# Embedding lookup, two interaction layers and a small MLP: a third low part by the adding DMA, 14 tiles split, rows in DRAM by chunks, second top weights loaded late

## The reference

```
x1[b,o,d] = relu(sum_{h,m} W1[o, 32h+m] * e[b,h,d] * e[b,m,d] + b1[o])        o < 128; h, m < 32
x2[b,o,d] = relu(sum_{h,m} W2[o, 32h+m] * x1[b,h,d] * e[b,m,d] + b2[o])       h < 64; m < 32
z = [sum_d x1[b,64:128,d], sum_d x2[b,:,d]], joined with the 16 dense inputs: 208 numbers
y = relu(relu(z W_top1 + b_top1) W_top2 + b_top2) W_top3
```

## Time and profile before

| | |
|---|---|
| median of 3 runs | 2021.38 us |
| profiled execution | 2020.18 us |
| its span, first to last instruction | 2018.4 us |
| PE busy | 1991.0 us, 99% |
| DVE busy | 1920.1 us, 95% |
| ACT busy | 1671.3 us, 83% |
| POOL busy | 1370.3 us, 68% |
| DMA, mean rate | 239 GB/s, 482.57 MB |

### The profile page before, as it was taken

The page is one execution under the profiler, slowest core; times in us unless marked ns, Lnnn a source line. Parts: engine busy times, 40 slices in busy tenths (PEclk is TensorE's granted clock), DMA queues, the critical chain, the costliest instruction groups (busy, mean ns, idle before and its releaser), DMA issues.

```text
span 2018.4 us, 24272 instructions
## 1 busy us (share of the span) xinstructions
PE 1991.0 (99%) x7030; PEld 1322.2 (66%) x7030; DVE 1920.1 (95%) x672; ACT 1671.3 (83%) x4953; POOL 1370.3 (68%) x647
## 2 busy tenths in 40 slices
PE   5999999999999999999999999999999999999999
PEld 3666666666666666666666666666666666666664
DVE  6999999999999999999999999999999999999992
ACT  3888888888888888888888888888888888888884
POOL 5767867777677767768667668677767768677520
PEclk9999999999999999999999999999999999999999
DMA  7999999989989999999999999999999999998960
GB/s 214 261 262 245 263 239 243 259 240 243 258 240 243 254 244 243 252 247 242 250 250 241 249 252 240 248 251 241 249 251 239 247 253 240 247 254 240 244 174 11
DMA packets 272119, 482.57 MB, mean 239 GB/s; under 512 B 37473, under 2 KB 70753, under 8 KB 271858
## 3 DMA queue, kind: packets, MB, share of 16 engines
q1 hardware_dynamic: 244786, 404.58, 66.7%
q0 software_dynamic: 26624, 75.52, 21.7%
q10 hardware_dynamic: 576, 0.92, 0.1%
HBM read 313.10 MB, written 16.78 MB: 163 GB/s over the span
## 4 chain that ended last, share of the span: by engine, by line
PE 97%; DMA 1%; POOL 1%; issue 0%; SPq 0%; ACT 0%; DVE 0%; POOLq 0%; ACTq 0%
PE acc L618 21%; PE acc L630 19%; PE acc L637 19%; PE acc L631 19%; PE acc L642 16%; PE acc L621 1%; POOL gathered L272 0%; DMA plo_dma<-pnear 0%; PE x1p L721 0%; PE acc L721 0%; DMA gathered<-in_tables,idx_all 0%; DMA x1rep<-x 0%; DMA near<-emb_rows 0%; PE acc L728 0%; PE x1p L600 0%
## 5 line engine op out<-in xcount | busy, mean ns | idle before, releaser
L305 POOL TENSOR_TENSOR prod<-near,h 128x2048 f32<-128x2048 f32 x126 | 581.5, 4615 | 442.3 <-DMA near<-emb_rows 287.7
L630 PE MATMUL acc<-phi,w2lo 128*128 128x512 f32 x1664 | 704.4, 423 | 0.9 <-ACT phi L838 0.9
L631 PE MATMUL acc<-phi,w2hi 128*128 128x512 f32 x1664 | 651.8, 392 | 0.0
L534 DVE TENSOR_TENSOR pnear<-near,x1p 128x2048 f32<-128x2048 f32 x254 | 568.8, 2282 | 3.2 <-DMA plo_dma<-pnear 3.1
L527 DVE TENSOR_TENSOR pfar<-far,x1p 128x4096 f32<-128x4096 f32 x128 | 565.3, 4417 | 0.0
L272 POOL DMA_INDIRECT gathered<-in_tables,idx_all x256 | 495.5, 1935 | 71.5 <-issue 68.2
L845 ACT CAST phi<-pfar 128x2560 fp32r<-128x2560 f32 x128 | 300.2, 2345 | 216.5 <-PE acc L631 183.6
L618 PE MATMUL acc<-prod,w1T 128*128 128x512 f32 x1024 | 460.2, 592 | 1.5 <-DVE prod L507 1.5
L538 DVE TENSOR_TENSOR plo<-pnear,phi 128x3072 fp32r<-128x3072 f32 x128 | 433.5, 3386 | 0.0
L538 DVE TENSOR_TENSOR plo<-pfar,phi 128x2560 fp32r<-128x2560 f32 x128 | 361.7, 2826 | 41.1 <-ACT phi L845 40.7
L630 PEld LDWEIGHTS acc<-phi,w2lo 128*128 128x128 f32 x1664 | 313.1, 188 | 96.5 <-issue 30.4
(11 more groups left out here) (77 smaller groups left out, 1258.6 us busy)
## 6 DMA issues: line engine op xcount, KB each, us to landing
far<-emb_rows SPq DMA_DIRECT2D x512, 256.0 KB, 4.1
near<-emb_rows SPq DMA_DIRECT2D x510, 256.0 KB
plo_dma<-pnear POOLq DMA_DIRECT2D x128, 512.0 KB
x1rep<-x SPq DMA_DIRECT2D x255, 256.0 KB
h<-emb_rows SPq DMA_DIRECT2D x128, 256.0 KB
emb_rows<-gathered SPq DMA_DIRECT2D x127, 128.0 KB
rem_parts<-rem_hi SPq DMA_DIRECT2D x128, 64.0 KB
gathered<-in_tables,idx_all POOLq DMA_INDIRECT x256
```

What stands on the lines that cost most here:

```text
L305: nc.gpsimd.tensor_tensor(prod1[:, :, :], near[(u + 2) % 3][:, :, :], h0[odd][:, :].unsqueeze(1).to_broadcast([P, K1, N]), ALU.mult).then_ ...
L534: return nc.vector.tensor_tensor(pnear[:, a, :, :], near[u % 3][:, :, :], factor.unsqueeze(1).to_broadcast([P, K1, N]), ALU.mult)
L630: nc.tensor.matmul(acc2[s][:, :], w2lo[:, t, :], phi[:, t, :], start=(t == T_DMA), stop=False)
L631: mm = nc.tensor.matmul(acc2[s][:, :], w2hi[:, t, :], phi[:, t, :], start=False, stop=(t == T_SPLIT - 1))
```

## The change

1. T_DMA goes from 2 to 3: the adding DMA makes three low parts (768 KB of additions instead of 512 KB). T_SPLIT goes from 13 to 14, T_WHOLE from 3 to 2: one more far tile is split. DVE still makes 11 low parts, now 5 near and 6 far.
2. `emb_rows` becomes [128 chunks][64 rows][512]. A chunk's rows are neighbours, so the four tiles of `near` are one transfer whose 128 rows are 8 KB long, and so are the four of `far`; the shift in `near` and `far` is now f + k + 4q.
3. A pair's store goes to two chunks: the destination's first dimension is 2, then 64 rows of 1 KB. The lookups' order on the partitions is turned to fit (`ids_f` in two copies, `table_row` in two transfers, issued by ACT).
4. With that order the remainder's pieces lie elsewhere: `rem_b`, `rem_prod`, `rem_hi`, `rem_lo` have 96 partitions instead of 64, and `place_remainder` has six transfers of 32 KB instead of three of 64 KB.
5. `wt2` gives up its own space; its 512 KB are loaded into `h0` at step 126 by two transfers, instead of at step 3.

```diff
+        emb = nc.dram_tensor("emb_rows", [CHUNKS, CHUNK], fp32, kind="Internal")     # CHUNK = 2*F*N
-T_DMA = 2
+T_DMA = 3
-T_SPLIT = T_FAR + 1
+T_SPLIT = T_FAR + 2

         def store_copy(eng, f0, pair, s):
-            dst = bass.AP(emb, f0 * ROW + pair * (2 * N), [[ROW, F], [PAIR_GATHERS * D, GS], [1, PAIR_GATHERS * D]])
+            dst = bass.AP(emb, pair * (2 * CHUNK) + f0 * N, [[CHUNK, 2], [PAIR_GATHERS * D, P // 2], [1, PAIR_GATHERS * D]])
             eng.dma_start(dst, gathered[s][:, :, :]).then_inc(emb_stored, 16)

-        def load_near_tiles(eng, col, s3, ks):
-            for k in ks:
-                src = bass.AP(emb, SH * k * ROW + col, [[ROW, F], [ROW, SH], [1, N]])
-                eng.dma_start(near[s3][:, k, :], src).then_inc(near_in[s3], 16)
+        def load_near_tiles(eng, c, s3):
+            src = bass.AP(emb, c * CHUNK, [[N, F], [SH * N, SH], [1, K1 * N]])
+            eng.dma_start(near[s3][:, :, :].rearrange("p k n -> p (k n)"), src).then_inc(near_in[s3], 16)

-            def load_far(col, s):
-                for k in range(K2):
-                    src = bass.AP(emb, SH * (K1 + k) * ROW + col, [[ROW, F], [ROW, SH], [1, N]])
-                    sp.dma_start(far[s][:, k, :], src).then_inc(far_in[s], 16)
+            def load_far(c, s):
+                src = bass.AP(emb, c * CHUNK + HALF * N, [[N, F], [SH * N, SH], [1, K2 * N]])
+                sp.dma_start(far[s][:, :, :].rearrange("p k n -> p (k n)"), src).then_inc(far_in[s], 16)

-                sp.dma_start(rem_b[:, :, :], gathered[s][HALF * GS:F * GS, :, :]).then_inc(rem_b_in, 16)
+                sp.dma_start(rem_b[:, :, :], gathered[s][REM:P, :, :]).then_inc(rem_b_in, 16)

                 for b, part in enumerate((rem_hi, rem_hi, rem_lo)):
-                    home = rem_parts[pair % 2][b * REM:(b + 1) * REM, :].rearrange("r (w n) -> r w n", w=2)
-                    sp.dma_start(home.bitcast(fp32), part[:, :].bitcast(fp32)).then_inc(rem_in, 16)
+                    for u in range(2):
+                        home = rem_parts[pair % 2][b * REM + u * HALF:b * REM + (u + 1) * HALF, :].rearrange("r (w n) -> r w n", w=2)
+                        sp.dma_start(home.bitcast(fp32), part[u * 2 * REM:u * 2 * REM + REM, :].bitcast(fp32)).then_inc(rem_in, 16)

+                if at == CHUNKS - 2:
+                    sp.wait_ge(p1_ready, CHUNKS)
+                    for s in range(2):
+                        src = a["W_top2"].rearrange("(s k p) n -> s p k n", s=2, p=P)[s]
+                        sp.dma_start(h0[s][:, :].rearrange("p (k n) -> p k n", n=HID2), src).then_inc(wt2_in, 16)

-            dve.wait_ge(ids_in, 32)
-            nc.vector.tensor_copy(ids_f[:, :, :].rearrange("r g (f q) -> r g f q", q=GS),
-                                  ids_n[:, :, :, :].rearrange("r q g f -> r g f q")).then_inc(ids_float, 1)
+            dve.wait_ge(ids_in, 48)
+            for w in range(2):
+                last = nc.vector.tensor_copy(
+                    ids_f[:, :, w * P // 2:(w + 1) * P // 2].rearrange("r g (f q) -> r g f q", f=F),
+                    ids_n[:, w * GS // 2:(w + 1) * GS // 2, :, :].rearrange("r q g f -> r g f q"))
+            last.then_inc(ids_float, 1)
```

More of the change, by code:

```diff
@@ L22 @@
 PAIR_GATHERS = 2 * CB // GS
-ROW = B * D + 1024
 SH = P // F
+CHUNK = 2 * F * N
 HALF = F // 2
 REM = 2 * HALF
+REM_ROWS = P - REM
 K1 = HALF // SH
@@ L82, in build_dlrm @@
         far = [sb(f"far_{s}", [P, K2, N]) for s in range(2)]
[L85 to L88, removed]
+        rem_b = sb("rem_b", [REM_ROWS, PAIR_GATHERS, D])
+        rem_prod = sb("rem_prod", [REM_ROWS, PAIR_GATHERS * D])
+        rem_hi = sb("rem_hi", [REM_ROWS, PAIR_GATHERS * D], fp32r)
+        rem_lo = sb("rem_lo", [REM_ROWS, PAIR_GATHERS * D], fp32r)
         rem_parts = [sb(f"rem_parts_{s}", [3 * REM, N], fp32r) for s in range(2)]
@@ L103, in build_dlrm @@
         wt1b = sb("wt1b", [P, HID1])
-        wt2 = sb("wt2", [P, HID1 // P, HID2])
         wt3 = sb("wt3", [P, HID2 // P])
@@ L123, in build_dlrm @@
         w1staged = pfar[:, 1, 0, :]
+        wt2 = [h0[k // 2][:, (k % 2) * HID2:(k % 2 + 1) * HID2] for k in range(M1)]
         hid1 = [near[2][:, :, :], near[0][:, :, :]]
@@ L130, in build_dlrm @@
         top_in = sem("top_in")
+        wt2_in = sem("wt2_in")
         ids_in = sem("ids_in")
@@ L193, in build_dlrm @@
         STORES = 16 * 2
-        LOADS = 16 * (1 + K1)
+        PLACES = 16 * 3 * 2
+        LOADS = 16 * 2
         SMALL_DMAS = 3
-        TOP_DMAS = 7
+        TOP_DMAS = 6
         def diagonals(wide, shift, row0=0):
             base = wide[:, 64 * row0 + shift:64 * row0 + shift + 1]
-            return bass.AP(base.tensor, base.offset, [list(base.ap[0]), [SH, K1], [65, F], [1, SH]])
+            return bass.AP(base.tensor, base.offset, [list(base.ap[0]), [1, K1], [65, F], [SH, SH]])
         def in_tiles(staged):
@@ L378, in _ @@
             load_h0(sp, 0, 0, 0)
-            load_near_tiles(sp, 0, 0, range(0, K1 // 2))
-            load_near(sp, N, 1, 1)
+            load_near(sp, 1, 1, 1)
             store_rows(1, 1, 1)
@@ L428, in step @@
                         sp.wait_ge(emb_stored, STORES * (pair + 3))
-                    load_near(sp, (c + 3) * N, 1 - odd, u % 3)
+                    load_near(sp, c + 3, 1 - odd, u % 3)
                 if not odd and within(at, 5):
@@ L434, in step @@
                     sp.wait_ge(pfar_ready, c + 1)
-                    load_far((c + 2) * N, odd)
+                    load_far(c + 2, odd)
                 if at == 3:
                     load_top()
+                if at == CHUNKS - 2:
[3 more added lines that the diff above has]
+                        sp.dma_start(h0[s][:, :].rearrange("p (k n) -> p k n", n=HID2), src).then_inc(wt2_in, 16)
             all_steps(step)
@@ L473, in _ @@
             for u in range(2):
-                hi0, lo1, hi2 = (w1rem[u][:, b * REM + u:(b + 1) * REM:2] for b in range(3))
+                hi0, lo1, hi2 = (w1rem[u][:, b * REM + u * HALF:b * REM + (u + 1) * HALF] for b in range(3))
                 nc.vector.tensor_copy(hi0, w16hi[:, :].bitcast(fp32))
@@ L554, in step @@
                     dve.wait_ge(x1p_ready, 1)
-                dve.wait_ge(far_in[odd], 16 * K2 * (turn * (U // 2)) + 16 * K2 * (u // 2 + 1))
+                dve.wait_ge(far_in[odd], 16 * (turn * (U // 2)) + 16 * (u // 2 + 1))
                 if begun(at):
@@ L676, in step @@
                     pe.wait_ge(p1_ready, c + 3)
-                    pe.wait_ge(rem_in, 48 * (pair + 2))
+                    pe.wait_ge(rem_in, PLACES * (pair + 2))
                     pe.wait_ge(z1_ready, c + 1)
@@ L720, in top2 @@
                     for k in range(M1):
-                        mm = nc.tensor.matmul(TOP_ACC[n][:, :], wt2[:, k, m * P:(m + 1) * P],
+                        mm = nc.tensor.matmul(TOP_ACC[n][:, :], wt2[k][:, m * P:(m + 1) * P],
                                               hid1[h][:, k, :], start=(k == 0), stop=(k == M1 - 1))
@@ L730, in top3 @@
                 mm.then_inc(y_mm, 1)
+            pe.wait_ge(wt2_in, 32)
             top2(0)
@@ L770, in remainder_hi @@
                 if pair:
-                    act.wait_ge(rem_in, 48 * pair)
+                    act.wait_ge(rem_in, PLACES * pair)
                 nc.scalar.copy(rem_hi[:, :], rem_prod[:, :]).then_inc(rem_hi_ready, 1)
+            for w in range(2):
+                nc.scalar.dma_start(table_row[w * P // 2:(w + 1) * P // 2, :],
+                                    a["table_rows"].rearrange("(f w q) one -> w f q one", w=2, q=GS // 2)[w]).then_inc(ids_in, 16)
             act.wait_ge(ident_ready, 1)
@@ L787, in _ @@
             act.wait_ge(emb_stored, STORES)
-            load_near_tiles(nc.scalar, 0, 0, range(K1 // 2, K1))
+            load_near_tiles(nc.scalar, 0, 0)
             remainder_hi(0)
```

21 lines of the change are left out of this document (9 added, 12 removed).

## The result

The changed kernel takes 2242.26 us (median of 4 runs, 2236.12 to 2244.3) against 2020.81 us in the same job: ratio 1.1093, 95% interval 1.1077 to 1.1108, slower by 221 us. The forecast was 2172 us, in a range from 2000 to 2300. The measured time lies in the range, 70 us above the forecast; the cause that the forecast gave, stores on two DMA engines, accounts for 18 of the 221 us.

The account below looks back on a forecast made before the run. PE was taken to bound the kernel before at 15.19 us per chunk, two DMA engines the changed one at 16.4 (14.8 + 2.7 - 1.1). 2020.2 + 126 x (16.4 - 15.19) = 2172 us, range 2000 to 2300.

Parts of the forecast that it names:

- PE: TensorE's matmuls: splitting one more tile takes 0.17 us off each chunk, period 15.02, at most 21 us in all.
- DVE: Low parts stay 11 tiles, so DVE's busy time stays 14.82 us per chunk: no cost, but the next bound.
- ACT: One more tile to round and negate: +0.95 us per chunk, 13.9 of 15.02, fitting into idle time; no cost.
- DMA, all engines: Work of all 16 engines per chunk: 13.97 + 1.54 - 0.75 + 0.05 = 14.8 us of 15.02, share 0.985.
- Long rows taken as a gain of 0.75 us: Loads of near and far with 8 KB rows run at 410 GB/s instead of 358: -0.75 us per chunk.
- Three more issues for the remainder go into what that frees: SP's queue: three more remainder issues, about 0.6 us each, fit into time freed by fewer near and far issues.
- DMA, the stores: A pair's stores lie on two engines: +2.7 us per chunk there, 17.5, less 1.1 of replication relief, 16.4.
- How that reaches PE: Late near holds POOL's multiply and the adding DMA behind it; DVE, with 0.2 us left, waits before pnear.
- signs of being right: Period about 16.4, PE idle, longer POOL and DVE waits, DMA share below 0.92, stores alone at about 0.12.
- A: Rival: stores spread as before, DMA's 14.8 below 15.02, PE stays the bound; 1999 us, 1.1% faster; chance 0.17.
- B: Rival: stores spread, 8 KB rows gain nothing, all DMA engines bound at 15.55 per chunk; 2066 us; chance 0.10.
- C: Rival: stores on two engines but absorbed, period 15.02 to 15.25; 1999 to 2028 us; chance 0.10.

Follow-up runs that it names:

- e5c: The changed kernel with 13 tiles split, two added tiles, stores over 16 engines, and near and far in four transfers each with 2 KB rows: 2109.06 us, ratio 1.0425.
- e12: The kernel before with only the third added tile and 14 split tiles, plus the late load of wt2: 2061.09 us, ratio 1.02.
- experiment 5: Changed kernel with 13 tiles split and stores over 16 engines, near and far reloaded with shorter rows: 2 KB 2109.06 us, 4 KB 2137.64, against 8 KB 2164.11.
- experiment 1: The changed kernel with each store spread over all 16 DMA engines again, one transfer per chunk: 2224.07 us, ratio 1.0998.
- e4: The kernel before with two more 128 KB stores per pair to an unread tensor, destination beginning with 2: 2035.6 us, ratio 1.009.
- e14: The kernel before with two more 128 KB stores per pair to an unread tensor, destination beginning with 32: 2020.93 us, ratio 1.0004.

## Why the prediction was right in the number and wrong in the cause

That the time lay in the range is in good part luck. All of the forecast's 152 us came from the stores on two engines, which cost 18; the other 203 us came from steps that the prediction put at nothing, at a gain, or only as load on those two engines.

The loss, taken apart along one path of runs (ratios, in points of a per cent): six transfers 3.7; from there to the rows by chunks with 2 KB rows (e5c, which also has the 96 partitions, the new order of the lookups, the stores' new form and the late `wt2`) 0.5; few transfers with rows of 8 KB 3.0; third tile 2.8; stores on two engines 0.9. These sum to 10.9, as they must along any path. Another path gives other parts, because parts that lengthen the same loops don't simply add: the third tile costs 40, 60, 83 or 114 us by what it is added to, the two-engine stores 18, 16 or -36.

- **PE**, -0.17 us per chunk: not to be seen, since PE no longer sets the pace in any kernel with 14 tiles. It can win 21 us at most, and never did.
- **DVE**: right. It is busy 1934.0 us in the whole run for 1920.1 before, 0.1 us more per chunk: 14.9 for 14.82. **ACT** too: 1782.5 for 1671.3 us is 0.87 more per chunk, for 0.95.
- **DMA, all engines**: forecast 14.8 us per chunk, measured 0.85 x 16.94 = 14.4. The rate of 8 KB rows was right (407 for 410). The third tile costs less work than taken, +1.2 for +1.54: POOL's queue took 26.6% of 2240.2 us, which is 596, for 21.7% of 2018.4, which is 438: 158 us more in 128 chunks. The window's 193 GB/s would make it +1.0 (786 KB in 4.07 us for 524 KB in 3.08), and e12's whole share has +0.9; the queue's total covers the whole run.
- **Long rows taken as a gain of 0.75 us**: the rate is gained, the time is lost, 55 us (2109 to 2164). The step counted work and not when things land: near landed no earlier after its first issue (experiment 5), and DVE waited longer for the adding DMA, 81 for 35 us in 1000.
- **"Three more issues for the remainder go into what that frees"**: the step that failed most on the kernel before, 75 us for nothing forecast. SP's time is freed at near and far, behind the replication; the new issues stand ahead of it, where SP's waits for ACT (97 us in 1000, 0.9 us in the pair shown) were the slack that they used up.
- **DMA, the stores**: right that two engines carry them (0.13), wrong that they are the bound. +2.7 us per chunk was forecast to become +1.2 in the period; measured are 0.14 us (18 us) in the changed kernel and 0.12 (16 us) alone. SP does wait for their landing, 92 us in 1000, but without that wait (7.0 in experiment 1) it waits elsewhere. Why the sum of the two engines' work overstates is open: its durations are those of engines that run all at once, as for the replication, and the relief may be larger than the two thirds taken, but no run shows it.
- **How that reaches PE**: the path through POOL and the adding DMA, named as the one with hardly any cover, is what the chains of the changed kernel and of e12 and DVE's waits show. There the place was right and the origin wrong. The six transfers act through SP's queue and the replication, which the prediction didn't name.

Most of the prediction's signs of being right came: PE idle, longer waits of POOL for near and of DVE for the adding DMA, a DMA share below 0.92, a stretch with stores at 0.13 (the period is 16.94, not 16.4, and layer 1 no longer stands in the chain). All but the stores' share would follow from anything that makes these landings late. So they couldn't tell this cause from others; experiment 1 did.

Rivals of the prediction: A fell with the 0.13 and with experiment 1 (spread, and still 2224 us). B, all engines full, is refuted by shares of 0.85 and, with the stores spread as B has it, 0.87. C (two engines, but absorbed) came nearest to the truth about the stores, though not about the time.

One rival was not tested: the clock. TensorE's granted clock is 0.976 on average in the changed kernel and 0.999 before; at the full clock PE's work would take some 50 us less, an estimate from that mean over 2240 us. PE has 4% of the chain and is idle for 186 us, so little of it can be expected in the time, but no run holds the clock.

No version that ran beat the kernel before.

## What to carry to other kernels

Where several engines have 0.2 to 1.5 us left per period, adding up each resource's work doesn't find the bound: follow the loop through the in-order queues, and ask of every issue that is added what stands behind it in its queue, not how long it takes. A queue's slack lies where the profile shows it waiting, and issues ahead of that point use it up; check that the chain closes on itself and compare its length with the old bound's. For a transfer that someone waits for, ask when it lands and not only at what rate it runs: here longer rows in fewer transfers raised the rate, landed no earlier themselves, and made another engine wait longer for the transfer of another queue. And take causes out one at a time before believing a sum that came out near.

## What the runs showed of the hardware that I had not expected

- A transfer whose destination begins with a dimension of 2 runs on two engines (share 0.13), but 262 KB per pair sent that way cost only 0.9% (e4), and nothing when spread (e14).
- Two transfers of 64 rows of 8 KB reach 238 GB/s at a full share, one of 128 rows 407, in one window each.
- The adding DMA is somewhat faster per byte with 6 KB rows than with 4 KB, 193 GB/s for 170 in one short window each; over the whole run the third tile took its queue 1.2 us more per chunk, where 170 GB/s would be 1.54.
- PE's mean clock over 1000 us was below its full level only in kernels in which PE waits: 0.97 in the changed kernel, 1.00 before. In the second row below, PE has waited for the adding DMA most of the time, at the full level of 2.4 GHz; in the first, just after, it is busy at half of it, 1.2 GHz:

```profile
1003.20:1006.20 3.00, 3.00 (x9) 2.32 (x8) 3.00 (x2) 1.99 (x2) 0.74 (x1) 0.50 0.89 169
999.00:1002.80 3.80, 1.12 (x5) 0.85 (x5) 0.91 (x1) 0.00 (x0) 3.40 (x1) 1.00 0.72 222
```
